# Gate logits from fp16 row parts turned by DMA transposes, and x loaded into the sum's buffer and added from the bank

## What is computed

```python
x = x + attention(layernorm(x))          # 16 heads of 16, causal, W_qkv, W_out with biases
x = x + ffn(layernorm(x))
# ffn(r): r + sum over the two chosen experts
xn = layernorm(r) * gamma + beta
probs = softmax(xn @ gate_w)             # 256 x 8
w, idx = top_k(probs, 2); w = w / sum(w)
h = gelu(xn @ w1[e] + b1[e])             # 256 -> 1024, exact gelu
out = sum_e cw[e] * (h @ w2[e] + b2[e])  # 1024 -> 256
```

## Time and profile before

| what | us |
|---|---|
| median of three runs | 972.66 |
| lowest, highest | 967.0, 973.46 |
| the profiled execution | 973.39 |
| its span in the trace | 971.6 |
| TensorE busy | 844.1 |
| VectorE busy | 702.2 |
| ScalarE busy | 572.8 |

### The profile page before, as it was taken

One profiled execution on the slowest core, in us unless ns is written; L12 is line 12 of the kernel. 1 busy time (PEld: TensorE's weight loads), 2 busy tenths in 40 slices (PEclk: granted clock), 3 DMA queues, 4 the chain that ended last, 5 costly groups with the idle time before them and its releaser, 6 DMA issues.

```text
span 971.6 us, 21008 instructions
## 1 busy us (share of the span) xinstructions
PE 844.1 (87%) x6760; PEld 555.8 (57%) x6760; DVE 702.2 (72%) x1566; ACT 572.8 (59%) x1048; POOL 468.5 (48%) x575
## 2 busy tenths in 40 slices
PE   4899988677797878787888797989989999999996
PEld 2555433233243424242434695869868888888875
DVE  6677888668669798979885585756756766656664
ACT  1767476546868787869776372545534445445453
POOL 4100033233535757657566556566566554554441
PEclk9999988779888979898997898989999999999998
DMA  8888667746767767576726884435535444444331
GB/s 202 253 274 270 235 190 195 194 113 170 206 195 204 184 188 198 163 200 179 203 75 208 169 145 69 58 79 98 79 55 79 79 78 73 76 76 83 52 73 23
DMA packets 185048, 139.40 MB, mean 143 GB/s; under 512 B 98065, under 2 KB 167569, under 8 KB 184817
## 3 DMA queue, kind: packets, MB, share of 16 engines
q1 hardware_dynamic: 153444, 95.16, 38.4%
q0 software_dynamic: 15776, 18.95, 12.3%
q10 hardware_dynamic: 15724, 23.95, 7.7%
HBM read 83.63 MB, written 44.80 MB: 132 GB/s over the span
## 4 chain that ended last, share of the span: by engine, by line
PE 54%; DVE 16%; DMA 13%; issue 5%; SPq 5%; ACT 3%; another core or an unknown queue 1%; POOL 1%; POOLq 0%; ACTq 0%; DVEq 0%
PE banks L776 18%; PE banks L794 18%; PE banks L598 5%; DMA weighed_values<-arena 3%; PE banks L715 3%; DVE arena L1239 3%; DMA inverse_sums<-arena 3%; DVE weights L1401 2%; PE banks L701 2%; PE banks L588 2%; PE banks L657 2%; SPq L1817 2%; DVE arena L1241 1%; SPq L1815 1%; DMA out<-arena 1%
## 5 line engine op out<-in xcount | busy, mean ns | idle before, releaser
L995 ACT ACTIVATE arena<-banks,arena 128x256 f32<-128x256 f32 (+1 forms) x312 | 152.4, 541 | 206.4 <-issue 95.7
L776 PE MATMUL banks<-arena,weights 128*128 128x256 f16 (+1 forms) x1872 | 210.9, 268 | 16.3 <-issue 15.7
L794 PE MATMUL banks<-weights,arena 128*128 x1704 | 198.2, 275 | 5.4 <-DVE arena L1531 3.1
L776 PEld LDWEIGHTS banks<-arena,weights 128*128 x1872 | 175.8, 99 | 45.5 <-issue 20.7
L1738 POOL DMA_INDIRECT out<-arena x71 | 117.0, 1648 | 159.1 <-DVE arena L1542 108.0
L794 PEld LDWEIGHTS banks<-weights,arena 128*128 128x128 f16 x1704 | 166.0, 99 | 31.1 <-issue 9.0
L657 PE MATMUL banks<-arena 64*128 64x128 f16 (+3 forms) x512 | 118.9, 330 | 32.8 <-ACT arena L931 9.3
L1529 DVE TENSOR_SCALAR arena<-arena 128x512 f16<-128x512 f32 (+1 forms) x156 | 76.9, 493 | 75.5 <-ACT arena L995 63.7
L629 PE MATMUL banks<-arena 62*128 62x384 f16 (+3 forms) x512 | 93.9, 326 | 32.5 <-DVE arena L1242 11.1
L1531 DVE SCALAR_TENSOR_TENSOR arena<-arena 128x512 f16<-128x512 f32 (+1 forms) x156 | 110.1, 706 | 5.6
L657 PEld LDWEIGHTS banks<-arena 64*128 64x128 f16 x512 | 38.0, 99 | 118.7 <-issue 36.3
(11 more groups left out here) (199 smaller groups left out, 1259.9 us busy)
## 6 DMA issues: line engine op xcount, KB each, us to landing
weights<-in_L_ffn_w ACTq DMA_DIRECT2D x16, 1024.0 KB, 7.6
arena<-in_L_ffn_w SPq DMA_DIRECT2D x32, 512.0 KB
qk_parts<-weights SPq DMA_DIRECT2D x64, 128.0 KB
arena<-qk_parts SPq DMA_DIRECT2D x128, 64.0 KB, 3.5
weighed_values<-arena SPq DMA_DIRECT2D x32, 256.0 KB
token_rows<-arena SPq DMA_DIRECT2D x12, 512.0 KB, 4.3
arena<-qk_parts SPq DMA_DIRECT2D x128, 32.0 KB, 3.5
arena<-weighed_values SPq DMA_DIRECT2D x32, 128.0 KB
```

The costliest lines, as they stand in the source:

```text
L776: m = pe.matmul(bank[:, c * TILE:c * TILE + WIDTH[j]], w1[:, k, wp, f:f + P], xp[:, k, 0:WIDTH[j]], start=(i == 0), stop=(i == len(terms) ...
L794: m = pe.matmul(bank[:, c * D:(c + 1) * D], hp[:, f, c * P:(c + 1) * P], w2[:, f // (FC // 2), wp, f % (FC // 2), :], start=(f == 0 and i ...
L995: m = act.activation(h_32[r % 2][:, c, 0:WIDTH[j]], banks[:, 1 + c2, c * TILE:c * TILE + WIDTH[j]], ACT.Gelu, bias=b1_now[j % 2][:, 2 * c2 ...
```

## The change

The gate now reads the fp16 high and low parts of the rows, which DMA transposes turn, and uses a gate_w split into a high and a low fp16 part with a power-of-two scale. Four DMA transposes a batch (`turn_rows`) write `rows_T`, which lies over the fp32 `rows`, dead by then. turn_x, copy_x and copy_out go. The row parts get a buffer of their own in place of `turned`. x is loaded again into `x2`, add_out adds the projection to it straight from the bank, 12 ticks earlier, and is what frees the bank. gate moves 42 ticks back; choose of the last two batches 36.

```diff
-            for k in range(KC):
-                at(base + 331 + 14 * k, "turn_x", (b, k))
-                at(base + 336 + 14 * k, "copy_x", (b, k))
-            at(base + 372, "gate", b)
-            at(base + 377, "copy_gate", b)
-            base += 48 if b < B - 2 else 0
+            for tt in range(TT):
+                at(base + 350 + 12 * tt, "turn_rows", (b, tt))
+            at(base + 414, "gate", b)
+            at(base + 419, "copy_gate", b)
+            base += 48 if b < B - 2 else 36
...
                 at(base + 175 + 12 * half, "out_proj", (b, half))
-                at(base + 181 + 12 * half, "copy_out", (b, half))
-                at(base + 193 + 12 * half, "add_out", (b, half))
+                at(base + 181 + 12 * half, "add_out", (b, half))
...
-        turned = a2.take(KC * T, k=KC, t=T)
+        row_parts = a2.take(TT * D, t=TT, d=D)
...
+        rows_T = rows.rearrange("p t d -> p (t d)").bitcast(F16).rearrange("p (k t) -> p k t", k=2 * KC)
...
+            elif stage == "out_proj":
+                freed["out_added"] += 1
+                side[(stage, n)] = (len(uses), len(side) + 1)
+                uses.append(((stage, n), ("add_out", n), "out_added", freed["out_added"]))
...
             def gate(b):
-                w.wait_ge(*side_out("turn_x", (b, 1)))
-                w.wait_ge(sem("x_scaled"), 1)
+                w.wait_ge(sem("rows_turned"), 16 * TT * (b + 1))
+                w.wait_ge(sem("scales"), 1)
                 bank = take_side("gate", b)
                 for tt in range(TT):
-                    for k in range(KC):
-                        m = pe.matmul(bank[:, tt * E:(tt + 1) * E], turned[:, k, tt * P:(tt + 1) * P], gate_w[:, k, :],
-                                      start=(k == 0), stop=(k == KC - 1))
+                    for i in range(2 * KC):
+                        m = pe.matmul(bank[:, 2 * E * tt:2 * E * (tt + 1)], rows_T[:, i, tt * P:(tt + 1) * P],
+                                      gate_parts[:, i % KC, :, :].rearrange("p s e -> p (s e)"),
+                                      start=(i == 0), stop=(i == 2 * KC - 1))
...
             def scale_rows(b, tt):
                 w.wait_ge(sem("shifts"), b + 1)
+                if b > 0:
+                    w.wait_ge(sem("side_made"), side_made("gate", b - 1))
...
             def split_rows(b):
                 w.wait_ge(sem("beta_added"), b + 1)
-                w.wait_ge(sem("acc_out"), 16 * (b + 1))
+                if b > 0:
+                    w.wait_ge(sem("rows_out"), 16 * b)
+                    w.wait_ge(sem("rows_turned"), 16 * TT * b)
...
             def add_out(b, half):
                 w.wait_ge(sem("x_again"), 16 * (b + 1))
-                w.wait_ge(*side_out("out_proj", (b, half)))
-                if b > 0:
-                    w.wait_ge(sem("rows_out"), 16 * b)
-                else:
-                    w.wait_ge(sem("v_store1"), 16 * (B // 2))
+                w.wait_ge(sem("side_made"), side_made("out_proj", (b, half)))
                 own_x = slice(2 * half, 2 * half + 2)
-                v.tensor_tensor(x2[:, own_x, :], turned[:, half, :].rearrange("p (s d) -> p s d", s=2), rows[:, own_x, :],
-                                ALU.add).then_inc(sem("out_added"), 1)
+                v.tensor_tensor(x2[:, own_x, :], side_bank("out_proj", (b, half)).rearrange("p (s d) -> p s d", s=2),
+                                x2[:, own_x, :], ALU.add).then_inc(sem("out_added"), 1)
...
                 if step == 0:
                     w.wait_ge(*side_out("gate", b))
+                    choose_at[0] = own.mark(both(logit, logit_parts[:, :, 0, :], logit_parts[:, :, 1, :], ALU.add))
...
+            def turn_rows(b, tt):
+                w.wait_ge(sem("row_low"), b + 1)
+                sp.dma_start(rows_T[:, :, tt * P:(tt + 1) * P], row_parts[:, tt, :].bitcast(F16),
+                             transpose=True).then_inc(sem("rows_turned"), 16)
...
             def load_again(b):
                 if b > 0:
-                    w.wait_ge(sem("side_made"), side_made("turn_x", (b - 1, 1)))
-                    w.wait_ge(sem("row_low"), b)
+                    w.wait_ge(sem("acc_out"), 16 * b)
                 else:
                     w.wait_ge(sem("spare_acc"), 16)
-                sp.dma_start(rows, t["L0_attn_x"][b].rearrange("(t p) d -> p t d", p=P)).then_inc(sem("x_again"), 16)
+                    w.wait_ge(sem("v_store1"), 16 * (B // 2))
+                sp.dma_start(x2, t["L0_attn_x"][b].rearrange("(t p) d -> p t d", p=P)).then_inc(sem("x_again"), 16)
```

More of the change, by code:

```diff
@@ L155, in build @@
         gate_w = keep.take(KC * E, k=KC, e=E)
+        gate_parts = keep.take(KC * 2 * E // 2, F16, k=KC, s=2, e=E)
         minus_half = keep.take(2 * TT, n=2, t=TT)
@@ L203, in build @@
         sums = [a2.take(HG * TT) for _ in range(2)]
-        turned = a2.take(KC * T, k=KC, t=T)
+        row_parts = a2.take(TT * D, t=TT, d=D)
         x2 = a2.take(TT * D, t=TT, d=D)
+        a2.at = -(-a2.at // 8) * 8
         rows = a2.take(TT * D, t=TT, d=D)
         scratch = rows[:, 0, :]
-        row_high, row_low = (x2[:, :, i * D // 2:(i + 1) * D // 2].bitcast(F16) for i in range(2))
+        row_high, row_low = (row_parts[:, :, i * D // 2:(i + 1) * D // 2].bitcast(F16) for i in range(2))
+        rows_T = rows.rearrange("p t d -> p (t d)").bitcast(F16).rearrange("p (k t) -> p k t", k=2 * KC)
         W_AT = a2.at
@@ L224, in build @@
         one_more = a2.take(TT)
+        logit_parts = a2.take(TT * 2 * E, t=TT, s=2, e=E)
         logit = a2.take(TT * E, t=TT, e=E)
@@ L463, in build @@
         BANKS_A_UNIT = len(E_USES)
-        TAKEN_BY = {"top_turn": "top_copy", "out_proj": "copy_out", "turn_x": "copy_x", "gate": "copy_gate",
-                    "count": "copy_count"}
-        uses, side, freed = [], {}, {"act_freed": 0, "exped": 0}
+        TAKEN_BY = {"top_turn": "top_copy", "gate": "copy_gate", "count": "copy_count"}
+        uses, side, freed = [], {}, {"act_freed": 0, "exped": 0, "out_added": 0}
         for stage, n in timetable:
@@ L953, in gap_exp @@
                 act.activation(gap, gap, ACT.Exp).then_inc(sem("gate_exp"), 1)
-            def copy_out(b, half):
-                w.wait_ge(sem("side_made"), side_made("out_proj", (b, half)))
-                if b > 0:
-                    w.wait_ge(sem("side_made"), side_made("gate", b - 1))
-                act.copy(turned[:, half, :], side_bank("out_proj", (b, half))).then_inc(sem("act_freed"), 1)
             def copy_gate(b):
                 w.wait_ge(sem("side_made"), side_made("gate", b))
+                w.wait_ge(sem("scales"), 1)
                 if b > 0:
                     w.wait_ge(sem("chosen"), b)
-                act.copy(logit, side_bank("gate", b)[:, 0:TT * E].rearrange("p (t e) -> p t e", t=TT)).then_inc(
-                    sem("act_freed"), 1)
+                act.activation(logit_parts.rearrange("p t s e -> p (t s e)"), side_bank("gate", b)[:, 0:TT * 2 * E],
+                               ACT.Copy, scale=UNDO_GATE).then_inc(sem("act_freed"), 1)
             def copy_count(b):
@@ L1207, in find_scales_2 @@
                 w.wait_ge(own.sem, m)
-                m = own.mark(both(S_TOP[:, 3:4], S_TOP[:, 3:4], S_TOP[:, 4:5], ALU.add))
+                m = own.mark(both(S_TOP[:, 3:4], S_TOP[:, 3:4], S_TOP[:, 5:6], ALU.add))
+                exponent, up = S_TMP[:, 0:5].bitcast(I32), S_TMP[:, 5:10].bitcast(I32)
                 w.wait_ge(own.sem, m)
-                m = own.mark(v.tensor_scalar(S_TMP[:, 0:4].bitcast(I32), S_TOP[:, 0:4].bitcast(I32), 23, None,
-                                             ALU.logical_shift_right))
+                m = own.mark(v.tensor_scalar(exponent, S_TOP[:, 0:5].bitcast(I32), 23, None, ALU.logical_shift_right))
@@ L1223, in find_scales_2 @@
+                m = own.mark(v.tensor_scalar(S_UNDO.bitcast(I32), exponent, 23, None, ALU.logical_shift_left))
                 w.wait_ge(own.sem, m)
+                m = own.mark(v.tensor_scalar(gate_parts[:, :, 0, :], gate_w, SCALE_GATE, None, ALU.mult))
                 v.tensor_scalar(gamma, gamma, SCALE_X, None, ALU.mult)
[L1225 to L1226 removed]
+                v.tensor_scalar(beta, beta, SCALE_X, None, ALU.mult).then_inc(sem("x_scaled"), 1)
@@ L1227, in find_scales_2 @@
+                w.wait_ge(own.sem, m)
+                v.scalar_tensor_tensor(gate_parts[:, :, 1, :], gate_w, SCALE_GATE, gate_parts[:, :, 0, :], ALU.mult,
+                                       ALU.subtract)
+                v.tensor_tensor(UNDO_GATE, S_UNDO[:, 2:3], S_UNDO[:, 4:5], ALU.mult)
                 v.tensor_tensor(UNDO_1, S_UNDO[:, 0:1], S_UNDO[:, 2:3], ALU.mult)
@@ L1960, in sync @@
                     turn_tokens(n)
+                elif stage == "turn_rows":
+                    turn_rows(*n)
                 elif stage == "table":
```

55 lines of the change are left out of this document (16 added, 39 removed).

## The result

The changed kernel took 993.92 us, median of four runs (990.77 to 1000.73), against 973.06 of the kernel before in four runs on the same chip (967.0 to 976.53): a ratio of 1.0225, interval 1.0184 to 1.0266. It is slower by 21 us, where I had forecast 8. The direction holds, and the range from 956 to 1000 too; the forecast's own range, 970 to 990, is missed by 4 us, and the size is two and a half times too small. The result lies between the forecast and rival 2 (1003). The profiled execution took 990.77 us around a span of 989.0.

The account below looks back on a forecast made before the run. VectorE was taken to bound attention, TensorE the expert stage. Terms -6 + 10 + 4 + 2.5 - 3.5 + 1.5 = +8.5 on 973.4 us, less 0.7, gave 981 us; own range 970 to 990, whole range 956 to 1000.

Parts of the forecast that it names:

- rival 2: Attention: the gate waits for its DMA transposes, landing in 8.26 us, 22 us more; 1003 us, chance 0.18.
- A: Attention, around row_high: turn_x, its two copies and the wait on acc_out go; -6 us, bounds 2 and 8 of gain.
- D: VectorE gets eight logit adds and sixteen adds from a bank in place of SBUF per batch; +2.5 us.
- B: Attention's projection: add_out waits for x landing in x2 and holds the bank, delaying half 1; +10 us, bounds -11 and +20.
- Rival 1: Attention: x lands in time, under 4.5 us, so add_out does not wait; faster, 958 us, chance 0.26.
- C: Attention: four DMA transposes a batch on SP's queue delay top_in; nothing counted for the gate; +4 us, bounds 0 and 10.
- E: Expert stage: batches 6 and 7 lose gate and transpose time on TensorE; -3.5 us, bounds -4.5 and -2.
- F: Transition, 520 to 541 us: batch 5's transposes stand before the first expert tile's; +1.5 us, bounds 0 and 4.

Follow-up runs that it names:

- run 12: Kernel before with top_in of every unit issued from ScalarE's queue: 978.17 us, ratio 1.0 to the kernel before on that chip.
- run 1: Changed kernel with load_again, the load of x, 18 ticks earlier (base + 148 in place of 166): 981.85 us, ratio 1.0101.
- run 5: Changed kernel with load_again at base + 148 and no DMA transposes, the gate reading unturned row parts: 968.06 us, ratio 0.9958.
- run 3: Changed kernel without its DMA transposes, the gate reading unturned row parts, x at its late tick: 982.66 us, ratio 1.0138.
- Run 7: Changed kernel with add_out of half 0 at base + 186 in place of 181, behind the maxima: 993.48 us, ratio 1.0245.
- run 8: Kernel before, unchanged, executed once more for a second profile: 977.87 us.
- run 4: Changed kernel with x loaded for batch 0 only, later add_outs waiting for the sum's store: 986.91 us, ratio 1.0176.
- run 6: Changed kernel with load_again at base + 148 and gate 12 ticks later, copy_gate and the last two batches' choice moved too: 988.34 us, ratio 1.0187.
- runs 9 to 11: Changed kernel, load_again at base + 148, plus top_in from ScalarE's queue, transposes behind top_in, or both: 984.84, 983.8, 984.97 us; ratios 1.006, 1.007, 1.006.
- run 10: Changed kernel with load_again at base + 148, transposes behind top_in on SP's queue, gate and choice later: 983.8 us, ratio 1.007.

## Why the prediction was right in direction and too small

The two profiled executions differ by 17.4 us, where the sum had 8.5. Unit 30 comes 11.3 us late (the sum's A to D: 10.5), the transition loses 6.2 (1.5) and the expert stage 0 (-3.5). So attention as a whole came out within a microsecond, and what is missing lies behind it. That counts from the start of the span. From unit 6 on attention lost 17.0 us, but run 12 shows that this mark is no firm ground: a kernel as fast as the one before reached it as early as the changed one and lost 8 us behind it.

Attention splits by the marks of the runs. Unit 30 stands at 538.4 us in the kernel after, 528.7 in run 1, 519.8 in run 5 and 527.1 before: 9.7 for x, 8.9 for the transposes, -7.3 for the rest. Counted from unit 6 on it would be 10.9, 11.3 and -5.3 (330.1, 319.2, 307.9, 313.1). The order matters too. With the transposes taken out first (run 3, unit 30 at 532.6) they have 5.8 and x has 12.7. So each share is known to 3 us or so, and a total near the forecast is in part luck: the transposes cost more and the rest gained more.

**B, the bank and x: right in mechanism and, as far as the marks tell, in size.** Forecast +10, measured 9.7 to 12.7. TensorE's half 1 comes 2.0 us later a batch, forecast 2.4. Two errors cancelled. The load lands faster than I took: 5.7, 4.9, 5.3, 4.8, 5.5 and 4.8 us from issue to add in six batches, not 6.85. But it is issued later against half 0 than in my sum, which had the two together: in the example 1.9 us after half 0 begins at 433.21. Run 7 speaks to what I had put side by side, VectorE's queue and the bank: only the bank shows a price. Rival 1 (x in time) is out, since the add waited for x in seven batches.

**C, the transposes in attention: too small, and by another way than I had said.** I gave them +4 for top_in and nothing for the gate, with a gate that waits as rival 2, 1003 us. Measured are 5.8 to 8.9, inside my bounds of 0 and 10 (8.2 to 11.3 from unit 6 on). But top_in is not where they cost in the changed kernel. TensorE waited 3.9 us for it there and 6.5 before, in the two views of waits:

```profile
PE banks L662 <- DMA arena<-arena: 3.9, 4, 1.9
```

```profile
PE banks L657 <- DMA arena<-arena: 6.5, 7, 2.7
```

They cost in part by the issue ahead of x, which the sum has in B: without them TensorE's wait for the add is 11.2 us shorter (run 3). The gate waits 0.2 us, as forecast, and for the reason given: x's lateness brings TensorE to it after the transposes have landed. With x in time (run 1) the gate waits 11.5 us in all and top_in 7.7. So C and B are not separate terms, and taking one away uncovers a part of the other. Issue (median 1.27 us) and landing (2.7 to 4.6 us in run 1) were as taken, so rival 2's 8.26 us did not occur there. The Trainium skill ("VectorE: DVE Perf Modes", "The three transpose paths") gives 1309 ns for a 128x128 block by DMA, by estimate 5.2 us for a transfer of four. In run 1 the last transfer had landed sooner in each of the five batches, which agrees with the rows by which I had set that figure aside. No run timed a single block.

**A and D: too small together.** A at -6 and D at +2.5 make -3.5; what is left in run 5, with neither cost, is -5.3 to -7.3. VectorE's add from the bank takes 0.69 us, forecast 0.75; the gate 0.56, forecast 0.57.

**E, the expert stage: right in work, open in time.** The expert stage by stretch, first the kernel before (the line of sums), then the changed one:

```profile
sum 430.10, PE 406.74 PEld 351.26 DVE 276.61 ACT 202.95 POOL 228.17; mean PE 406.74 PEld 351.26 DVE 276.61 ACT 202.95 POOL 228.17
```

```profile
559.00:989.00 430.00, 401.94 (x3686) 346.46 (x3686) 277.86 (x753) 200.12 (x416) 228.57 (x196) 0.97 0.47 80
```

TensorE's work fell by 4.8 us (forecast 4.0) and its idle time grew by 4.7. But the second profile of the kernel before (run 8) took 433.4 us for this stage:

```profile
sum 433.40, PE 407.44 PEld 351.82 DVE 277.33 ACT 203.00 POOL 227.96; mean PE 407.44 PEld 351.82 DVE 277.33 ACT 203.00 POOL 227.96
```

Its idle time is 26.0 us, against 23.4 and, in the changed kernel, 28.1. Against that profile the changed kernel gains 3.4 us, the forecast. So the stage gained between 0 and 3.4 us, and no more can be said. In the changed profile one wait of 2.08 us for a tile's transposes at 606.47 is new. More idle time also stands beside GpSimd's slot scatters, which I had left open at 5 us either way: 8.5 us between 599 and 622, where the kernel before had 4.6 between 581 and 601. The 11.62 us of the earlier trace rows were no full stop either: TensorE was busy 7.00 of the 11.60 us from 585.7 on.

**F, the transition: the term that was mis-sized, beyond its bounds.** Forecast +1.5, bounds 0 and 4; measured +6.2, with 14.4 and 14.6 us in the two profiles before. This is the step that failed by most: I had counted three transposes of 0.72 us of engine time ahead of the first tile's, and no time for an issue that doesn't go through. What happens is that SP stands in the issue of a transpose for 12.25 us, just behind the 3 MB of late weights, with the DMA engines full, and all that SP issues later waits with it. My first reading of the result was that x(6), issued behind those weights, was the cause. Run 1 says no: x in good time, transition 20.3. Runs 3 and 5 say what it is: without the transposes 16.1 with x late, and 14.7 with x early. So of 6.2 us some 5 are the transposes'. The mark scatters as well: 18.1 us in run 4, and 16.5 in run 12, which has none of the change.

So the forecast lacks +5 in F, +5 in C and +3.5 in E, the last within scatter, with 4 the other way in A and D. The last 3.5 us to the median's 21 are mostly scatter: the profiled execution was the fastest of its four.

The signs I had named: the add waiting for x in five or six of eight batches (seven), TensorE waiting for the add (16.0 us), ScalarE down 19 (16.4) and TensorE 20 (13.2). TensorE waiting for top_in was no sign of the change, as shown above. The batches of attention grew from 52.7 to 55.3 us, counted from unit 2 to unit 26 (forecast 54 or 55). TensorE's shortfall may go with its clock: between 214 and 476 us its granted clock was 0.83 in place of 0.88 (1 is the 2.4 GHz level), with TensorE busy 196.7 of these 262 us in place of 215.3. Whether that clock takes part in the 17 us was not separated; run 1 has 0.83 too and is 12 us faster.

What stays open is how the transposes act in attention: by 5 us of issue on SP, or by traffic against top_in and the reads of qk_parts. The latter ended 17.7 us of waits in the changed kernel; before, they ended less than half of that:

```profile
PE banks L629 <- DMA arena<-qk_parts: 8.3, 4, 3.4
```

But that is no sign of the transposes' traffic: run 3, which has none, shows 17.5 us and run 12 shows 14.6.

```profile
PE banks L634 <- DMA arena<-qk_parts: 17.5, 7, 4.9
```

Moving the gate moved the wait (run 6), moving top_in or the transposes (runs 9 to 11) brought at most the difference between 1.010 and 1.006, which the intervals don't tell apart. The place on SP's queue is not the whole cause, since run 10 changed it and kept a ratio of 1.007, where run 5, without the transposes, has 0.9958; traffic was not tested by itself.

## What to carry to other kernels

An instruction that frees a bank must have every other input early: here a load 5 us late cost twice, on its own engine where nobody minded, and through the held bank where everybody did. When a wait disappears, or a new one appears, ask which other wait it covers: taking away x's lateness or the transposes gave 12 and some 11 us, both together 26, and the profile of the changed kernel named only one of them. A mark inside the kernel is a fair start for counting only if it repeats between kernels that differ behind it: that of unit 6 did not. And follow each added transfer to the place where the queues are fullest, the handover between stages, rather than price it by a steady stretch.

## What the runs showed of the hardware that was not expected

The issue of a DMA transpose is not a fixed price: the group of the changed kernel reads 1188, 1266 and 12249 ns for the least, the median and the most, and the long one lies where the DMA engines are full, at a share of 1.05 between 545 and 550 us:

```profile
L1871 SPq DMA_TRANSPOSE arena<-arena x32: 1188/1266/12249, 267.0 to 691.1; - x32
```

A plain load of 512 KB landed in about 5 us in attention, at a DMA share of 0.7, and in 17.5 us behind 3 MB of weights. An addition that reads one operand from a bank costs 12 ns more in the mean for 512 columns than from SBUF (687 against 675; the medians are 692 and 682). The kernel with its loads of x taken away was no faster than with early ones, as far as four scattered executions tell (run 4); and the changed kernels, with run 12, which changes only a queue, reach unit 6 2 to 6 us sooner than the kernel before, which took 214 us in both its profiles. Neither is explained.
